# Moving the last stores of a projection stage into the program of the stage behind it

## The reference, cut to what matters

```python
x = x + attn(layernorm(x), ...)      # self-attention, 16 heads of 16, causal, relative bias
x = x + xattn(layernorm(x), ctx)     # cross-attention, 8 heads of 128, keys from ctx (4 x 1024 x 192)
x = x + ffn(layernorm(x), ...)       # channel mix with token shift
```

```python
q, k, v = xn @ Wq.T + bq, xn @ Wk.T + bk, xn @ Wv.T + bv      # per head
attn = q @ k.T * scale + M @ rel_bias @ M.T                    # M interpolates 32 to 512 positions
out = softmax(where(future, -inf, attn)) @ v
return out @ Wo.T + bo
```

## Time and profile before

| | us |
|---|---|
| median of three runs | 2642.66 |
| lowest, highest run | 2639.93, 2644.95 |
| the profiled execution, its own time | 2639.82 |
| its span in the profile | 2637.7 |
| TensorE, busy share of the span | 97% |
| granted TensorE clock, mean | 0.991 |

### The profile page before, as it was taken

How to read it: one execution, slowest core, us unless ns; L and a number is a source line. 1 busy time by engine, 2 the same in 40 slices (tenths; PEclk the granted TensorE clock), 3 DMA queues, 4 the chain that set the end, 5 groups by cost and what they waited for, 6 DMA issues and landing times. The chain is left out here.

```text
span 2637.7 us, 47104 instructions
## 1 busy us (share of the span) xinstructions
PE 2551.6 (97%) x17680; PEld 2291.6 (87%) x17680; DVE 1926.4 (73%) x3632; ACT 1608.6 (61%) x3051; POOL 138.3 (5%) x161
## 2 busy tenths in 40 slices
PE   7799979999999999999999999999999999999998
PEld 5699968998899889998999889988998899889987
DVE  6588867776777777776777677767776777677787
ACT  5699845566566646565556566556665556656566
POOL 2353010000000000000000000000000000000003
PEclk9899989999999999999999999999999999999999
DMA  7896442001200120003000200012001200110000
GB/s 220 222 191 143 94 157 80 17 16 65 73 17 16 47 82 17 21 12 119 18 17 17 107 31 17 16 57 73 17 24 57 73 17 16 64 67 17 28 1 33
DMA packets 93854, 156.54 MB, mean 59 GB/s; under 512 B 42576, under 2 KB 56080, under 8 KB 93680
## 3 DMA queue, kind: packets, MB, share of 16 engines
q1 hardware_dynamic: 89680, 141.20, 17.9%
q0 software_dynamic: 3248, 12.72, 1.6%
q10 hardware_dynamic: 752, 0.26, 0.0%
HBM read 122.56 MB, written 27.39 MB: 57 GB/s over the span
## 5 line engine op out<-in xcount | busy, mean ns | idle before, releaser
L1623 ACT CAST pt_hi<-xt_ps 128x512 fp32r<-128x512 f32 x1024 | 592.9, 585 | 568.2 <-PE xt_ps L1593 552.3
L1702 DVE TENSOR_TENSOR pt_lo<-xt_ps,pt_hi 128x512 fp32r<-128x512 f32 x1024 | 704.7, 688 | 255.2 <-ACT pt_hi L1623 251.7
L1691 DVE TENSOR_SCALAR_CACHE_REDUCE xprobs<-xs_ps 128x1024 f32<-128x1024 f32 x512 | 626.7, 1224 | 176.0 <-PE xs_ps L1533 171.5
L1604 PE MATMUL xo_ps<-pt_hi,v_hi 128*128 128x256 f32 x2048 | 647.4, 316 | 2.4 <-DVE pt_lo L1702 2.3
L1629 ACT ACTIVATE xprobs<-xprobs,xneg_max 128x1024 f32<-128x1024 f32 x512 | 591.4, 1155 | 27.3 <-DVE xneg_max L1697 27.3
L1593 PE MATMUL xt_ps<-ident,xprobs 128*128 128x128 f32 x4096 | 603.8, 272 | 0.0
L1604 PE MATMUL xo_ps<-pt_hi,v_lo 128*128 128x256 f32 x2048 | 571.3, 279 | 0.0
L1604 PE MATMUL xo_ps<-pt_lo,v_hi 128*128 128x256 f32 x2048 | 570.0, 278 | 0.0
L1593 PEld LDWEIGHTS xt_ps<-ident,xprobs 128*128 128x128 f32 x4096 | 484.1, 140 | 61.9 <-issue 6.7
L1604 PEld LDWEIGHTS xo_ps<-pt_hi,v_hi 128*128 128x128 f32 x2048 | 386.3, 189 | 5.8 <-DVE pt_lo L1702 2.6
L1604 PEld LDWEIGHTS xo_ps<-pt_lo,v_hi 128*128 128x128 f32 x2048 | 388.3, 190 | 2.0
(11 more groups left out here) (236 smaller groups left out, 2699.7 us busy)
## 6 DMA issues: line engine op xcount, KB each, us to landing
v_split<-ctx_split SPq DMA_DIRECT2D x68, 768.0 KB, 5.8
xq<-x_split SPq DMA_DIRECT2D x64, 512.0 KB, 3.3
q_st<-rel_split SPq DMA_DIRECT2D x32, 256.0 KB, 4.2
q_st<-q_split SPq DMA_DIRECT2D x32, 192.0 KB, 4.6
k_st<-k_split SPq DMA_DIRECT2D x32, 192.0 KB, 5.0
ctx_split<-ctx_out POOLq DMA_DIRECT2D x8, 768.0 KB, 4.1
q_split<-stage_hi SPq DMA_DIRECT2D x8, 512.0 KB, 4.7
k_split<-stage_hi SPq DMA_DIRECT2D x8, 512.0 KB, 4.8
```

Of the source, the lines that this page charges most:

```text
L1604: last = pe.matmul(o_ps[:, 0:GQ], v[:, vs], pt[:, c % 3, GQ * j:GQ * (j + 1)], start=c == 0 and j == 0 and m == 0, stop=c == PIECES - 1 an ...
L1623: act.copy(pt_hi[:, c % 3, :], t_ps[:, c % 3, :]).then_inc(t_rounded, 1)
L1691: dve.tensor_scalar(probs[:, par if kind == "A" else 1 - par, t, CHUNK * i:CHUNK * (i + 1)], s_ps[:, buf, :], LOGIT, None, ALU.mult, ALU.m ...
L1702: dve.tensor_tensor(pt_lo[:, c % 3, :], t_ps[:, c % 3, :], pt_hi[:, c % 3, :].bitcast(F32), ALU.subtract).then_inc(t_ready, 1)
```

## The change

The stores of units 10 to 15 are no longer issued by the first stage's SyncE program, and the wait at its end is gone. The attention's SyncE program issues them: units 10, 11 and 12 first; then, after step 0's scores, `load_stacks(3)` and unit 13; then `load_stacks(4)` and `load_v(2)` behind their waits; then units 14 and 15, `wo_raw` and `bo`; then the loop from n = 1 on. The wait for all stores stands ahead of `load_stacks(8)`, the first that reads tokens of the second batch. `stage_hi`, `stage_lo` and `rel_out` must outlive the first stage: they are now parts of `attn_late`, the half of the former `attn_t` for batches 2 and 3, which is written from step 16 on. The other half, `attn_early`, is placed where `attn_t` was. `store_hi` and `store_lo` issue the same transfers as before.

```diff
@@ decoder_layer
-                self_projections(nc, a, x, ident, v_split, q_split, k_split, rel_split, key_split, stacks)
-                attn_t = until_finish.enter_context(nc.sbuf_tensor("attn_t", [P, B, PAIRS, N], F32))
+                attn_late = until_finish.enter_context(nc.sbuf_tensor("attn_late", [P, B // 2, PAIRS, N], F32))
+                self_projections(nc, a, x, ident, v_split, q_split, k_split, rel_split, key_split, stacks, attn_late)
+                attn_early = until_finish.enter_context(nc.sbuf_tensor("attn_early", [P, B // 2, PAIRS, N], F32))
+                attn_t = (attn_early, attn_late)
@@ SelfStacks
+    SLOTS = 6
+    STORES = B * CH * 2
+    def store_hi(self, sp, n):
+        u = n % self.SLOTS
+        sp.dma_start(self.stored_to(n)[0], self.stage_hi[:, u, :].bitcast(F32).rearrange(
+            "p (a c) -> p a c", a=1).to_broadcast([P, 2, 512])).then_inc(self.stage_stored[u], 16)
+    def store_lo(self, sp, n):
+        u = n % self.SLOTS
+        sp.dma_start(self.stored_to(n)[1], self.stage_lo[:, u, :].bitcast(F32)).then_inc(self.stage_stored[u], 16)
@@ load_stacks
+        if n == PAIRS:
+            for s in range(self.SLOTS):
+                sp.wait_ge(self.stage_stored[s], 32 * len(range(s, self.STORES, self.SLOTS)))
@@ self_projections
+        lent = attn_late[:].rearrange("p b z c -> p (b z) c").bitcast(F32R)
+        stage_hi, stage_lo, rel_out = lent[:, 0:SLOTS], lent[:, SLOTS:2 * SLOTS], lent[:, 2 * SLOTS:2 * SLOTS + 4]
@@ self_projections, SyncE
-            for n in range(2 * EACH, TB * EACH):
+            for n in range(2 * EACH, stacks.STORES - SLOTS):
                 store(n)
-            for u in range(SLOTS):
-                sp.wait_ge(stage_stored[u], 32 * len(range(u, len(UNITS), SLOTS)))
@@ self_attention, SyncE
+            def store(n):
+                stacks.store_hi(sp, n)
+                stacks.store_lo(sp, n)
+
+            for n in range(stacks.STORES - stacks.SLOTS, stacks.STORES - 3):
+                store(n)
+            sp.wait_ge(scored, 3)
+            stacks.load_stacks(sp, 3)
+            store(stacks.STORES - 3)
+            sp.wait_ge(scored, 6)
+            stacks.load_stacks(sp, 4)
+            sp.wait_ge(weighed, 1)
+            stacks.load_v(sp, 2)
+            for n in range(stacks.STORES - 2, stacks.STORES):
+                store(n)
             sp.dma_start(wo_raw[:], a["WoT"].rearrange("(h p) o -> p h o", p=P)).then_inc(wo_loaded, 16)
             sp.dma_start(bo[:], a["bo"].rearrange("(a c) -> a c", a=1).to_broadcast([P, C])).then_inc(wo_loaded, 16)
-            sp.wait_ge(scored, 3)
-            stacks.load_stacks(sp, 3)
-            for n in range(STEPS):
-                if 2 <= n + 1 < STEPS:
+            for n in range(1, STEPS):
+                if 3 <= n + 1 < STEPS:
                     sp.wait_ge(weighed, n)
                     stacks.load_v(sp, n + 1)
```

More of the change, by code:

```diff
@@ L140, in __init__, with stored_to @@
         self.v_loaded = [sem(f"v_loaded{s}") for s in range(2)]
+        self.stage_stored = [sem(f"stage_stored{s}") for s in range(self.SLOTS)]
     def v_slots(self, u):
         return self.v_st[:, u].rearrange("p (k c) -> p k c", k=2)[:, :, 0:QI * P].rearrange("p k (j c) -> p k j c", c=P)
+    def stored_to(self, n):
+        tb, oh, w = n // (2 * CH), n // 2 % CH, n % 2
+        dest, hi_at, lo_at = ((self.splits[0], slice(0, 2), 2), (self.splits[1], slice(0, 3, 2), 1))[w]
+        rows, cols = slice(P * oh, P * (oh + 1)), slice(512 * tb, 512 * (tb + 1))
+        return dest[rows, hi_at, cols], dest[rows, lo_at, cols]
+    def store_hi(self, sp, n):
[5 more added lines that the diff above has]
+        sp.dma_start(self.stored_to(n)[1], self.stage_lo[:, u, :].bitcast(F32)).then_inc(self.stage_stored[u], 16)
     def load_keys(self, sp):
@@ L165, in load_v, with self_projections @@
                          self.v_split[:, QI * b:QI * (b + 1), at:at + SLOT_ROWS].bitcast(F32)).then_inc(self.v_loaded[u], 16)
-def self_projections(nc, a, x, ident, v_split, q_split, k_split, rel_split, key_split, stacks):
+def self_projections(nc, a, x, ident, v_split, q_split, k_split, rel_split, key_split, stacks, attn_late):
     with ExitStack() as ctx:
@@ L181, in self_projections @@
         TB = T // 512
-        SLOTS = 6
+        SLOTS = stacks.SLOTS
+        lent = attn_late[:].rearrange("p b z c -> p (b z) c").bitcast(F32R)
+        stage_hi, stage_lo, rel_out = lent[:, 0:SLOTS], lent[:, SLOTS:2 * SLOTS], lent[:, 2 * SLOTS:2 * SLOTS + 4]
+        stacks.stage_hi, stacks.stage_lo = stage_hi, stage_lo
         y = sb("y", [P, 8, C])
@@ L187, in self_projections @@
         w_hi, w_lo = sb("w_hi", [P, 3, CH, C], F32R), sb("w_lo", [P, 3, CH, C], F32R)
-        stage_hi, stage_lo = sb("stage_hi", [P, SLOTS, 512], F32R), sb("stage_lo", [P, SLOTS, 512], F32R)
         gamma, beta = sb("gamma", [P, CH]), sb("beta", [P, CH])
@@ L201, in self_projections @@
         lo_rows = sb("lo_rows", [P, 1])
-        rel_hi, rel_out = sb("rel_hi", [P, 3, N], F32R), sb("rel_out", [P, 4, N], F32R)
+        rel_hi = sb("rel_hi", [P, 3, N], F32R)
         banks = ctx.enter_context(nc.psum_tensor("banks", [P, 8, 512], F32))
@@ L212, in self_projections @@
         projected, stage_hi_ready, stage_lo_ready = sem("projected"), sem("stage_hi_ready"), sem("stage_lo_ready")
-        stage_stored = [sem(f"stage_stored{u}") for u in range(SLOTS)]
+        stage_stored = stacks.stage_stored
         v_done, v_hi_ready, v_lo_ready = sem("v_done"), sem("v_hi_ready"), sem("v_lo_ready")
@@ L255, in store @@
             def store(n):
-                tb, oh, w = UNITS[n]
-                u, rows, cols = n % SLOTS, slice(P * oh, P * (oh + 1)), slice(512 * tb, 512 * (tb + 1))
-                dest, hi_at, lo_at = ((q_split, slice(0, 2), 2), (k_split, slice(0, 3, 2), 1))[w]
                 sp.wait_ge(stage_hi_ready, n + 1)
-                sp.dma_start(dest[rows, hi_at, cols], stage_hi[:, u, :].bitcast(F32).rearrange(
-                    "p (a c) -> p a c", a=1).to_broadcast([P, 2, 512])).then_inc(stage_stored[u], 16)
+                stacks.store_hi(sp, n)
                 sp.wait_ge(stage_lo_ready, n + 1)
-                sp.dma_start(dest[rows, lo_at, cols], stage_lo[:, u, :].bitcast(F32)).then_inc(stage_stored[u], 16)
+                stacks.store_lo(sp, n)
             for n in range(2 * EACH):
@@ L616, in self_attention @@
         block = ctx.enter_context(nc.Block())
-        STEPS = B * PAIRS
+        STEPS, STEPS_EACH = B * PAIRS, B // 2 * PAIRS
         LOADS = 16 * 3
@@ L778, in store @@
                 act.wait_ge(weighed, n + 1)
-                act.copy(attn_t[:, n // PAIRS, n % PAIRS, :], o_ps[:]).then_inc(attn_stored, 1)
+                act.copy(attn_t[n // STEPS_EACH][:, n // PAIRS % 2, n % PAIRS, :], o_ps[:]).then_inc(attn_stored, 1)
             for n in range(-2, STEPS):
@@ L1069, in to_token_major @@
                         last = pe.transpose(a_ps[:, t % 2, P * p:P * (p + 1)],
-                                            attn_t[:, t // QI, p, P * (t % QI):P * (t % QI + 1)], ident[:])
+                                            attn_t[t // (2 * QI)][:, t // QI % 2, p, P * (t % QI):P * (t % QI + 1)], ident[:])
                     last.then_inc(token_major, 1)
```

## The result

| | kernel before | kernel after |
|---|---|---|
| median of 20 runs | 2643.86 us | 2638.78 us |
| lowest and highest | 2639.07 to 2648.61 | 2631.77 to 2644.51 |
| time of the profiled execution | 2639.82 | 2641.69 |
| its span | 2637.7 | 2639.6 |

The ratio is 0.9982, with an interval of 0.9974 to 0.9989: the change saves 4.8 us (2.9 to 6.9). That is a real gain, about half of the 8.5 forecast. It is just under 0.2%, so of my three outcomes it is the middle one, within 0.2% of no change, to which I had given 0.15; "faster by more" had 0.80. The time is inside the range on record (2629.5 to 2640), but above the forecast's own 2631 to 2637 and next to the 2639 of rival 2. Of the 4.6 us between 2638.78 and the forecast, 1.2 are the median of before, which was 2642.66 in the three runs shown; the other 3.4 are gain that was forecast and did not come.

What follows compares the result with a forecast made beforehand. TensorE, busy 97% of a 2637.7 us span, bounds the kernel, except a hole at the first stage's end set by store transfers. -9.0 + 0.5 = -8.5 us from median 2642.66 gives 2634.2; range 2629.5 to 2640, the forecast's own 2631 to 2637.

Steps and rivals of the forecast that it cites:

- rival 2: Attention: value and stack loads late by a few us, meeting POOL's traffic; 5 to 6 us lost, 2639; chance 0.14.
- faster by more: Whole kernel: outcome of a gain above about 0.2%, 5.3 us, so a time under 2637.4; chance 0.80.
- The stage end: End of first stage: without the last stores and their wait, attention starts at 77.8 to 78.1, not 86.9; -9.0 us.
- S: Start of the attention, TensorE's first score matmul; 87.1 us before, forecast near 78; later times counted from it.
- Rival 4: First stage's end: something else holds it, so it ends no sooner; gain under 5 us, 2640; chance 0.05.
- The value loads: Attention, v(2) and v(3): moved stores and POOL's earlier block delay them; +0.5 us stall, ends 0 and 2.
- Rival 3: Attention: three pairs of value loads land in 12.9 us, losing 16.5 us; +7.5 us overall, 2650.2; chance 0.05.
- The half clock at the start: Attention's start: TensorE again begins at 1.2 GHz; price taken as unchanged, 1 us to both sides.
- Rival 1: Attention's start: full clock returns early, at S+3; another 2.6 us gained, 2631.6; chance 0.10.
- The rest: POOL's delay hidden by 90 us; after 320 us all shifts as one piece, clock falls moving it 1 us either way.

Runs made afterwards that it cites:

- e1: The kernel after run once more with no edit, for a second profile; median 2637.74 us, ratio 0.9978 to the kernel before.
- e3: Kernel after, with POOL's context blocks begun only after step 4's weighing (four steps weighed); median 2639.76 us, ratio 0.9988 to the kernel before.
- e10: Kernel after with the edits of e2 and e3 together; median 2636.18 us, ratio 0.9970 to the kernel before.
- e4: Kernel after with 14 unused matmuls in TensorE's first-stage pause at 27 to 30 us; median 2636.74 us, ratio 0.9972 to the kernel before.
- e8: The kernel before once more with no edit, a single profiled execution; span 2638.8 us.
- e9: Kernel before with POOL's context blocks begun only after the first weighing, no store moved; median 2647.80 us, ratio 1.0004 to the unedited kernel.
- e13: Kernel before with POOL's context blocks begun only after the fourth weighing, no store moved; median 2644.45 us, ratio 1.0007 to the unedited kernel.
- e11: Kernel after with each POOL store waiting for a step's scores, one block in three steps; median 2634.43 us, ratio 0.9969 to the kernel before.
- e12: Kernel after with the edits of e2, e11 and e6 (both fillers) together; median 2629.36 us, ratio 0.9946 to the kernel before.
- e2: Kernel after with the stores of units 14 and 15 issued ahead of step 2's value load; median 2636.37 us, ratio 0.9973 to the kernel before.
- e5: Kernel before with the 14 unused matmuls of e4 in TensorE's first-stage pause; median 2639.12 us, ratio 0.9986 to the unedited kernel.
- e6: Kernel after with e4's filler plus 18 unused matmuls at the end of TensorE's first stage; median 2635.38 us, ratio 0.9971 to the kernel before.

## Why the prediction was right, and where not

**The stage end (-9.0): right.** In e1, at full clock in the first stage, S moved by 9.3 us. Nothing else took the stores' place: VectorE was last, at 77.35, for 77.5 foretold, the next block began 0.3 us behind it, ScalarE's longest wait for a slot was 6.6 us (6.8 in after) where it had been 6.5. Rival 4 falls.

**The value loads (+0.5, with ends 0 and 2): this is the term that was mis-sized.** The profiles show 2.2 and 2.3 us of late value loads in the kernel after. Three parts can be read off.
- v(3) was placed well: issued at S+26.3 in after (I had 26.6). I took the slower half's landing as 6.7 us, from the pair at 105.42, and a stall of 0.5. It landed in 7.4 and 7.8 us in the two profiles of after, with waits of 1.12 and 1.31. The pair at 105.42 had no load of stacks just ahead of it in SyncE's queue; v(3) now had, for the last transfer of load_stacks(5) was issued from 111.80 to 112.22 and v(3) from 112.27, and units 14 and 15 stood just before that; with POOL away but these in place it was 1.90 us late (e3), with both away it landed in 3.1 (e10).
- v(4) was not in the forecast's list (rivals 2 and 3 alone counted a third pair). It is issued while step 6's stacks and POOL's block (116.29 to 118.4 in after) are moving and lands in 9.4 us, 0.4 to 0.6 us late. I had followed the moved stores up to the last load that they pass in SyncE's queue and stopped there.
- The later waits, 0.5 us in each profile of after and up to 2.1 in e4. In the kernel before, the slowest loads of the attention landed in 7.1 to 7.7 us, and 7.4 was my figure for what a load can bear (7.7 was still borne in e8 and e9, and cost 0.17 us in the first profile of before). That row of before gave v(2) 0.7 us to spare, and I used it for v(2) alone. Other loads that met a POOL block had as little. I wrote that POOL would start 9 us earlier and that its delay was hidden by 90 us of slack; that is true of POOL's own work, and says nothing of whom it meets. e13 shows the price of another meeting, 3.4 us, and e11 and e12 that with POOL paced no load from step 4 on is late.

In sum the attention became 2.0 and 2.6 us longer in the two profiles of after, and 1.4 to 4.8 in the six variants short of e12, for the 0.5 taken. This is rival 2's mechanism, in the two profiles of after at about half of its price of 5 to 6 us; I had given it a chance of 0.14 and argued it chiefly for v(2) and v(3). That the time is inside my range, which reached up to rival 2's 2639 and a little beyond, is owed to that width and not to the forecast.

**The half clock at the start: right.** In e1 the clock is 0.50 from 78 to 90 us and 0.99 in 90 to 92, so it is back at S+12; before it was at S+10 (0.50 up to 97, and 0.99 in 97 to 107). Two more us at half clock cost at most 1, the margin that I gave. Rival 1 falls. The Trainium skill (TensorE: Matmul & The Clock Gate, Part 1: The HAM clock gate) says that sustained work brings the clock back. The traces agree only in part: e1's clock came back while TensorE was busy without a break from 86 to 90, but in after TensorE was busy for all of 32 to 46 us and the clock stayed at 0.50. What brings it back is not shown here.

**The rest: not settled.** Behind the attention the two profiles of after show 2318.8 and 2319.8, the before-type ones 2317.4 to 2318.5 and once 2320.3 (e13), and e2, e3 and e4, which share the shift, 2315.9 to 2317.0. It varies by 4.4 us with no order that I can name. My plus or minus 1 us for it was too narrow.

**The sum.** -9.3 + 2.0 to 2.6 is -6.7 to -7.3. The runs say -4.8 (2.9 to 6.9), and -5.8 (2.9 to 9.0) for e1. The rest, 1 to 2 us longer in both profiles of after, would make up for it, but three pairs of profiles with the same clock in 27 to 52 us, one of each kernel, speak against counting it to the change:

| pair | clock | S | attention | rest | span |
|---|---|---|---|---|---|
| e1 less before | 1.00 | -9.3 | +2.6 | +2.0 | -4.7 |
| e4 less e5 (filler in both) | 1.00 | -9.4 | +5.1 | -0.7 | -5.0 |
| after less e9 (POOL shifted in e9) | 0.66 | -8.7 | +1.9 | +0.3 | -6.4 |

The spans agree with the gain of the medians, the first term is nearly the same in all three, and the attention is longer in each, by 1.9 to 5.1 us. The rest goes both ways. So the longer attention is the part that every pair shows; how late the value loads are in the typical execution, three pairs don't say.

**Not foreseen: the first stage isn't fixed.** I took all before 77.5 us as given. In the ten profiles without a filler the clock in 27 to 52 us was 1.00 five times, 0.93 twice, 0.80 once and 0.66 twice, in kernels of both kinds; in the four with one it was 1.00 each time. The length of the pause alone does not order them: it was 2.9 to 3.2 us where the clock stayed up, 3.8 and 3.9 in the two long falls, but 2.5 to 2.8 in the three shorter ones. A fall to 0.66 costs 7.5 to 8.2 us (e9 against before, after against e1). The two groups of e9's runs, 8 to 10 us apart, and the smaller spread with a filler say that it makes much of the spread of 10 us in both kernels. It is why a single pair of profiles showed after 1.9 us slower while it is 4.8 us faster. Since both kernels pay it, it moves the difference of the medians little, as far as these runs tell.

**Rival 3** (16.5 us of late loads) needed landings of 10.4 us and more in three pairs; the longest in the two profiles of this kernel was 9.4 us.

**Open.** Why e9's shift of POOL made no wait and e13's did: the longest landing was 7.7 in the one and 8.7 and 9.6 in the other, so e9 was just inside, but what sets the landing of a load that meets a POOL block was not tried. The change also gave `stage_hi`, `stage_lo` and `attn_t` other places in memory; no run keeps the new places with the old order of stores. Nor does a run say why the clock falls in one execution and not in the next. A third slot for the values, which would give each load a step more, was not tried either.

## What to carry to other kernels

When transfers are moved out of a hole into a tight loop, list every load of the loop with its bearable landing time, not only those that the moved ones pass in their own queue: here loads with some tenths of a us to spare turned late when another engine's bulk transfers came at other moments, and in the two profiles of this kernel that ate a fourth of the 9.3 us. A bulk queue of another engine can be paced by the loop's own step counter, so that it meets the loads where they can bear it; here two profiles show that it worked, and no run shows what it is worth by itself. And before two profiles are compared, the granted clock should be compared stretch by stretch, also in stages that the change does not touch.

## What the runs showed of the hardware

- Behind TensorE's pause of 2.5 to 3.9 us between two projections, at 27 to 30 us, its clock falls to 1.2 GHz in some executions of one and the same kernel and not in others. In after it stays there for some 17 us, though TensorE is busy for all of the 14 us from 32 to 46. With fourteen unused matmuls in the pause it was at 1.00 in four profiles of four, and 12 runs spread over 6.9 us (e4) instead of 10.6 (e1); they cost nothing that a profile shows, and gained 3.7 us (1.3 to 5.8) in the kernel before.
- A 64 KB value load, two of them to a step, lands in 2.2 us at best (e11 and e13, several times) and in up to 9.8 us (e6; 9.7 in e4, the one that cost 2.10 us) when it meets a POOL block. POOL is not needed for a slow one: behind units 14 and 15 and the stacks alone it took 8.4 us (e3).
- Full clock at the start was not kept: in e6 it was lost again where TensorE waited for the first softmax (0.41 us of matmul in 2), and of the 2 to 3 us hoped for the profile shows 1.6. In e12 it fell later and for a shorter time, 0.91 over 76 to 96 us against 0.83; what made the difference was not tried.
